# Routing of two top-2 expert layers moved into the loops that make their inputs, with pair lists in DRAM and weights loaded per expert

## What is computed

```python
x = x + gnn0(norm(x))      # node softmax * row softmax of (h @ h.T masked by adj), times x @ weight, + bias
x = x + ffn0(norm(x))      # 8 experts, top 2 of x @ Wg + bg; silu(x @ w1) * (x @ w3) @ w2, hidden 512
x = x + gnn1(norm(x))      # relu((adj @ x) @ W.T + b)
x = x + ffn1(norm(x))      # 8 experts, top 2 of x @ gate_w.T; gelu(x @ w1.T + b1) @ w2.T + b2, hidden 1024
# routing of both expert layers:
top_vals, top_idx = top_k(logits, 2);  gates = softmax(top_vals)
y = sum over the two chosen experts of gate * expert(x)
```

## Time and profile before

| | us |
|---|---|
| median of 3 runs | 1865.2 (1862.47 to 1866.99) |
| the profiled execution, own time | 1865.87 |
| its span, first to last instruction | 1864.2 |
| TensorE's mean granted clock, of full speed | 0.927 |
| PE, DVE, ACT, POOL busy in the span | 1550.2, 1156.6, 639.2, 651.3 |
| PE instructions, DVE instructions | 9584, 3520 |

### The profile page before, as it was taken

The page is one execution under the profiler, slowest core; times in us unless marked ns, Lnnn a source line. Parts: engine busy times, 40 slices in busy tenths (PEclk is TensorE's granted clock), DMA queues, the critical chain, the costliest instruction groups (busy, mean ns, idle before and its releaser), DMA issues. The chain is left out here.

```text
span 1864.2 us, 35268 instructions
## 1 busy us (share of the span) xinstructions
PE 1550.2 (83%) x9584; PEld 1295.2 (69%) x9584; DVE 1156.6 (62%) x3520; ACT 639.2 (34%) x1367; POOL 651.3 (35%) x1336
## 2 busy tenths in 40 slices
PE   5899999999999718999996079999259999999990
PEld 4788888888888607888785045555138888888880
DVE  5466677776677685555653837666765655566543
ACT  2333333333333302333332523222014454454544
POOL 0123233222332105555553014333224444445530
PEclk9899999999999958999999579999669999999995
DMA  7224433344333171111112744655501111111119
GB/s 116 87 109 149 156 134 127 131 147 158 134 127 126 60 271 43 51 52 49 52 51 78 250 146 160 212 190 179 214 24 34 37 37 34 37 34 37 39 30 296
DMA packets 91017, 204.73 MB, mean 110 GB/s; under 512 B 13792, under 2 KB 64481, under 8 KB 87009
## 3 DMA queue, kind: packets, MB, share of 16 engines
q1 hardware_dynamic: 74368, 148.15, 23.8%
q0 software_dynamic: 11328, 30.95, 5.3%
q10 hardware_dynamic: 5280, 25.17, 3.4%
HBM read 146.17 MB, written 58.08 MB: 110 GB/s over the span
## 5 line engine op out<-in xcount | busy, mean ns | idle before, releaser
L1128 PE MATMUL bank<-ffn_w_in_parts,ffn_x_t 128*128 128x512 f32 x1416 | 359.7, 402 | 1.4 <-DVE ffn_w_in_parts L1254 1.4
L1152 PE MATMUL bank<-ffn_w_out_parts,ffn_hidden_t 128*128 128x256 f32 x2124 | 285.5, 289 | 26.2 <-DVE ffn_hidden_t L1244 26.2
L1128 PEld LDWEIGHTS bank<-ffn_w_in_parts,ffn_x_t 128*128 128x128 f32 x1416 | 259.2, 190 | 54.7 <-DVE ffn_w_in_parts L1254 4.4
L1152 PEld LDWEIGHTS bank<-ffn_w_out_parts,ffn_hidden_t 128*128 128x128 f32 x2124 | 264.2, 193 | 30.5 <-DVE ffn_w_out_parts L1254 19.2
L623 PE MATMUL bank<-h_t,attn_h_tile 128*128 128x512 f32 (+1 forms) x1092 | 248.9, 383 | 3.9 <-POOL attn_h_tile L492 3.9
L658 PE MATMUL bank<-support,attn_probs_t 128*128 128x512 f32 x650 | 246.6, 412 | 2.8 <-DVE attn_probs_t L532 2.6
L623 PEld LDWEIGHTS bank<-h_t,attn_h_tile 128*128 128x128 f32 x1092 | 196.9, 189 | 46.2 <-issue 4.1
L520 ACT CAST attn_probs_t<-bank 128x512 fp32r<-128x512 f32 (+1 forms) x182 | 98.7, 557 | 351.9 <-PE bank L632 351.9
L1194 ACT ACTIVATE ffn_silu_or_gelu<-bank,w_b_in 128x128 f32<-128x128 f32 x472 | 134.7, 368 | 202.4 <-PE bank L1139 202.4
L660 PE MATMUL bank<-support,attn_probs_t 128*128 128x256 f32 x676 | 184.9, 280 | 0.0
L1244 DVE TENSOR_TENSOR ffn_hidden_t<-ffn_silu_or_gelu,ffn_hidden_t 128x512 fp32r<-128x512 f32 x118 | 81.1, 692 | 138.3 <-ACT ffn_hidden_t L1200 123.0
(11 more groups left out here) (245 smaller groups left out, 2414.5 us busy)
## 6 DMA issues: line engine op xcount, KB each, us to landing
adj_tile<-in_adj SPq DMA_DIRECT2D x25, 1663.5 KB, 21.6
mask<-attn_mask ACTq DMA_DIRECT2D x26, 832.0 KB, 3.4
nbr_mask<-mask SPq DMA_DIRECT2D x26, 832.0 KB, 5.2
comb_y<-y SPq DMA_DIRECT2D x12, 768.0 KB, 10.3
w_w_in<-in_w SPq DMA_DIRECT2D x16, 512.0 KB, 10.3
w_w_in<-in_w_t SPq DMA_DIRECT2D x16, 512.0 KB, 4.3
comb_x<-x SPq DMA_DIRECT2D x6, 768.0 KB, 10.5
w_w_out<-in_w SPq DMA_DIRECT2D x1, 4096.0 KB, 20.0
```

The costliest lines, as they stand in the source:

```text
L1128: ins = pe.matmul(bank[2 + 2 * slot + b][:, :], XT[:, slot, xp, k, :], WIP[:, wp, k, b * CH:(b + 1) * CH], start=n == 0 and k == 0, stop=n ...
L1152: ins = pe.matmul(bank[7][:, 0:D], HTT[:, hp, k, :], WOP[:, wp, k, :], start=n == 0 and k == 0, stop=n == 2 and k == KH - 1)
```

## The change

Both `route` stages are removed. Their work is done per row tile by new methods of `Gate` inside `attend` and `neighbours`:

- `pick` (DVE): the top two of the 8 logits of a row by the 8-wide maximum and index instructions, and which experts the row uses.
- `count` (PE): two matmuls with 8 columns, the rank of each pair within its tile and the tile's totals; the result lies in a corner of bank 2 (attend) or 5 (neighbours).
- `rank` (DVE): adds the running base of each expert and takes out the two places of each row. An expert's list has room for all rows (`CAP`), so a place is known at once.
- `scatter` (POOL): two indirect DMAs of 128 pairs of integers, 8 bytes each, to the list `pairs` in DRAM.
- `plan` (DVE, once at the end): for each of the 59 tiles its expert and the row of `pairs` where it begins.

In `attend` PE's scores of chunk 2 wait for `ranks_read` and `count` stands at group 3 of a step. In `neighbours` `count` stands first in a step, ACT converts all four groups (`odd` moves from DVE), one bank less is used for the transposed sum, and the last step does `add` and `finish` ahead of the last logits. `experts` reads each tile's list with a small DMA by SP (a register load and a DMA per tile), and the weights are loaded there, expert by expert, by ACT, ahead of `copy_x(0)`; DVE waits for one expert's weights at a time (8 tiles are written out ahead of its loop). In ffn1 the first matrix is still loaded in `neighbours`. The empty lists are filled in `project`.

```diff
 class Gate:
+    def pick(self, dve, t, slot):
+        dve.wait_ge(self.logits_ready, t + 1)
+        dve.memset(self.TAKER[:, E + 1:E + 2], 0.0)
+        link(dve.max(self.M8[:, slot, :], self.L[:, slot, :]))
+        dve.tensor_tensor(self.r["gates"][:, 1, bass.ds(t, 1)], self.M8[:, slot, 1:2], self.M8[:, slot, 0:1],
+                          ALU.subtract).then_inc(self.diff_ready, 1)
+        link(dve.max_index(self.I8[:, slot, :], self.M8[:, slot, :], self.L[:, slot, :]))
+        link(dve.tensor_copy(self.EF[:, slot, :], self.I8[:, slot, 0:2]))
+        link(dve.tensor_scalar(self.OH[:, slot, :], self.k["IE"][:], self.EF[:, slot, 1:2], None, ALU.is_equal))
+        dve.scalar_tensor_tensor(self.USED[:, slot, :], ...).then_inc(self.used_ready, 1)
+    def count(self, pe, t, slot, rows=P):
+        pe.wait_ge(self.used_ready, t + 1)
+        pe.wait_ge(self.ranks_read, t)
+        pe.matmul(self.PS[:, 0:E], self.k["BEFORE"][0:rows, :], self.USED[0:rows, slot, :], start=True, stop=True)
+        pe.matmul(self.PS[:, E:2 * E], self.k["ONES"][0:rows, :], self.USED[0:rows, slot, :], ...).then_inc(self.ranked, 1)
+    def rank(self, dve, t, uses, slot):
+        dve.wait_ge(self.ranked, t + 1)
+        link(dve.tensor_tensor(self.A[:], self.PS[:, 0:E], base, ALU.add))
+        dve.tensor_tensor(self.BASE[:, 1 - slot, :], self.PS[:, E:2 * E], base, ALU.add).then_inc(self.ranks_read, 1)
+        for k in range(2):
+            link(dve.scalar_tensor_tensor(self.JUNK[:, k, :], ..., accum_out=self.SLF[:, slot, k:k + 1]))
+        dve.tensor_copy(self.SLI[:, slot, :], self.SLF[:, slot, :]).then_inc(self.slots_ready, 1)
+    def scatter(self, pool, t, uses, slot, rows=P):
...
+        for k in range(2):
+            pool.indirect_dma_start(out=self.pairs, out_offset=..., in_=self.VALS[0:rows, slot, k, :], ...)
+    def plan(self, dve):
...
@@ attend, DVE, step
                         rest(t, slot, [g])
                         ...
+                    gate.rank(dve, t - 2, uses - 1, slot)
                     if not (first and slot == 0):
                         gate.logits(dve, t - 1, 1 - slot)
+                        gate.pick(dve, t - 1, 1 - slot)
@@ attend, PE
+                        if c == 2 and (not known(t) or t >= 4):
+                            pe.wait_ge(gate.ranks_read, t - 3)
...
+                        if g == 3 and (not known(t) or t >= 2):
+                            pe.wait_ge(masked, T * NC if last else (t + 2) * NC)
+                            gate.count(pe, t - 2, slot)
-def route(nc, bank, name, LG, r, w, load):
...
@@ class Weights
+    def load(self, act):
         if self.b_in is not None:
+            act.dma_start(self.BI[:], self.b_in).then_inc(self.b_loaded, 16)
+            act.dma_start(self.BO[:], self.b_out.partition_broadcast(P)).then_inc(self.b_loaded, 16)
+        m = self.w_in.shape[2] // E
+        for e in range(E):
+            if not self.early:
+                act.dma_start(self.WI[:, :, e * m:(e + 1) * m], self.w_in[:, :, e * m:(e + 1) * m]).then_inc(self.in_loaded[e], 16)
+            act.dma_start(self.WO[:, :, e * D:(e + 1) * D], self.w_out[:, :, e * D:(e + 1) * D]).then_inc(self.out_loaded[e], 16)
@@ experts, SP
+                    row = sp.value_load(r["row"][0:1, bass.ds(t, 1)], min_val=0, max_val=LIST_TILES - 1)
+                    sp.dma_start(PAIRS[:, bass.ds(t * 2, 2)], pairs[bass.ds(row * P, P), :]).then_inc(pairs_in[slot], 16)
@@ experts, ACT
+                w.load(act)
                 copy_x(0, 0, 0)
@@ neighbours, POOL, step
+                        gate.scatter(pool, t - 3, uses - 2 + slot, 1 - slot)
                     gate.norm(pool, t, uses, slot)
```

More of the change, by code:

```diff
@@ L39 @@
 PAIR_ROWS = 2 * NP
+CAP = T * P
+LIST_TILES = 240
+assert LIST_TILES >= S + (E - 1) * (T - 1)
 def tiles(eng, count, step, head=2):
@@ L604, in _ @@
                 link(dve.tensor_scalar(NATT[:], NATT[:], NSM[:, 3:4], None, ALU.mult))
-                tiles(dve, T, step)
+                tiles(dve, T, step, head=4)
+                gate.rank(dve, T - 2, (T - 2) // 2, T % 2)
                 gate.sums(dve, T - 1, (T - 1) % 2, range(E))
                 gate.logits(dve, T - 1, (T - 1) % 2)
+                gate.pick(dve, T - 1, (T - 1) % 2)
+                gate.rank(dve, T - 1, (T - 1) // 2, (T - 1) % 2)
+                gate.plan(dve)
             @block.tensor
@@ L667, in _ @@
                 scores(0, 0, True)
-                tiles(pe, T, step)
+                tiles(pe, T, step, head=4)
+                gate.count(pe, T - 2, T % 2)
+                gate.count(pe, T - 1, (T - 1) % 2, TAIL)
 def combine(nc, a, bank, x_in, gates, x_out, parts):
@@ L1324, in _, with neighbours @@
                     split_w_in(1, 2, b)
-                tiles(dve, S, step)
-def neighbours(nc, a, bank, XH, gate_w, LG, w):
+                tiles(dve, S, step, head=E)
+def neighbours(nc, a, bank, XH, gate_w, r, w):
     sizes = (7, 7, 6, 6)
@@ L1392, in _, with step @@
                 gate.constants(pool)
-                tiles(pool, T, lambda t, uses, slot, first, last: gate.norm(pool, t, uses, slot))
+                def step(t, uses, slot, first, last):
+                    if not known(t) or t >= 3:
+                        gate.scatter(pool, t - 3, uses - 2 + slot, 1 - slot)
+                    gate.norm(pool, t, uses, slot)
+                tiles(pool, T, step, head=6)
+                gate.scatter(pool, T - 3, (T - 3) // 2, (T - 3) % 2)
+                gate.scatter(pool, T - 2, (T - 2) // 2, (T - 2) % 2)
+                gate.scatter(pool, T - 1, (T - 1) // 2, (T - 1) % 2, TAIL)
+                gate.scattered_all(pool)
             @block.tensor
@@ L1449, in _ @@
                 pe.wait_ge(w_loaded, 32)
-                tiles(pe, T, step)
+                tiles(pe, T, step, head=6)
             @block.scalar
@@ L1464, in even, with odd @@
                     act.activation(AT[:, 0, 0:w], bf[0][:, 0:w], ACT.Copy, bias=1.0, scale=1.0 / BIG).then_inc(at_ready, 1)
+                def odd(t, slot, g, first):
+                    act.wait_ge(flipped, t * G + g + 1)
+                    if not (first and slot == 0 and g < 2):
+                        act.wait_ge(used, t * G + g - 1)
+                    w = GS[g][1] * P
+                    act.activation(AT[:, 1, 0:w], bf[1][:, 0:w], ACT.Copy, bias=1.0, scale=1.0 / BIG).then_inc(at_odd, 1)
                 def tail(t, slot, first):
@@ L1475, in flip_out @@
                         act.wait_ge(out_done, t - 1)
[L1476 removed]
+                    act.copy(AGT[:, slot, :, :], bank[4][:, 0:D].rearrange("p (k n) -> p k n", k=KD)).then_inc(agt_ready, 1)
                 def step(t, uses, slot, first, last):
[L1479 to L1483 removed]
+                    very_first = first and slot == 0
+                    even(t, slot, 0, first)
+                    if not very_first:
+                        tail(t - 1, 1 - slot, first)
+                    odd(t, slot, 1, first)
+                    even(t, slot, 2, first)
+                    if not very_first:
                         flip_out(t - 1, 1 - slot, first)
+                    odd(t, slot, 3, first)
                     if last:
@@ L1574, in build @@
             w.place_out(while_used)
-            route(nc, bank, "gate0", LG, r, w, w.load)
-            experts(nc, a, bank, "ffn0", w, H0, r)
+            experts(nc, a, bank, "ffn0", w, H0, r, a["pairs"][0])
         with ExitStack() as while_used:
```

436 lines of the change are left out of this document (203 added, 233 removed).

## The result

The changed kernel took **1919.6 us** (median of 4 runs, 1917.9 to 1927.7), the kernel before 1863.8 beside it: ratio 1.031, 95% interval 1.0289 to 1.033 (the two medians by themselves give 1.030). It is 3.1% slower; 1856.5 was forecast, 1827 to 1880. The profiled execution has a span of 1916.2 us against 1864.2, so 52.0 us are to be found.

The account below looks back on a forecast made before the run. PE was taken to bound the attention loop and mostly the neighbour loop, DVE the route stages. Terms -13.3 - 11.4 + 7 + 9 = -8.7 us took 1865.9 to 1857.2, and the median 0.7 under it to 1856.5; range 1827 to 1880.

Parts of the forecast that it names:

- What throttles the issuer: Expert stages: a queue holds about 1690 rows, so ACT's weight issues take 26.2 us; first product at 27.4, in ffn1 25.4.
- Rival (a): Expert stages: ACT isn't held by its queue, first products come 15.3 and 13.6 us earlier than forecast; 1827.6 us, chance 0.13.
- The tail of attend: Last attention logits to first expert product: 10.4 us of work, a 0.96 barrier, then 27.4; product 13.3 us earlier than before.
- scatter lies beside plan: End of attend: POOL's last scatters, 2 x 1.03 us and a landing, about 4.5 us, run beside DVE's 5.2 us plan.
- The tail of neighbours: End of neighbours to ffn1's first product: rows end 2.8 us sooner, three tiles 18.4, plan 5.2; product 11.4 us earlier.
- What the attention loop pays: Attention loop: added PE work and waits 0.17 us, DVE stalls 0.1 us a tile, over 26 tiles +7 us.
- rival (b): Both routed loops pay next to nothing: count fits between transposes, DVE stays in its room; 1840.5 us, chance 0.12.
- PE's waits for the masked sum under 5 us: Attention loop, sign in the profile after: PE's waits for DVE's masked sum stay under 5 us in total.
- 2.25 us of room, and 0.54 of idle time before the result: Attention loop: DVE's slack, by which an odd step takes 2.8 us of added work for nothing, an even one 3.2.
- Rival (c): Both routed loops: DVE becomes the bound, its twelve added instructions cost 3.6 us a tile, 24 us in all; 1880, chance 0.25.
- the port, for POOL's scatters in neighbours: Neighbours loop: POOL's scatters exclude DVE instructions with two SBUF inputs and lengthen DVE's sums, one way to the 1880 us case.
- Expert loops, "nothing": Expert loops, combine and project: no added cost, as SP's list read runs ahead of the 5.4 us of a tile.

Follow-up runs that it names:

- e4_loads_spread: Changed kernel, with ACT's weight loads spread over its first steps (three experts ahead of the first copy) instead of all eight first: 1900.9 us, ratio 1.0209.
- e8_plan_late: Changed kernel, with DVE starting plan at the end of both routed loops only when POOL has issued the last two scatters: 1918.8 us, a single run.
- f3_full_rows: Changed kernel, with the last tile's scatters given 128 rows instead of 127, the 128th sent to two unread places: 1913.4 us, ratio 1.0261.
- e1_adj_ahead: Changed kernel, with the adjacency load issued one tile earlier in SP's order in the attention loop: 1877.3 us, ratio 1.0089.

## Why the prediction was wrong

Two steps failed: that a later result in attention costs nothing (39.7 us of the miss), and that the scatters at the end of both routed loops lie beside plan (7.2 and 8 us). By its own steps, in its order:

- **What throttles the issuer: right.** The queue of ACT, which no row had shown full, behaved like SP's. 26.0 us of issues against 26.2, product at 27.4 against 27.4; in the second stage 24.9 from ACT's first issue against 25.4. Rival (a) is out, and e4_loads_spread shows that the wait was ACT's and could be avoided.
- **The tail of attend: short by 7.2 us.** From the last logits to the plan 2.7 us (3.1 forecast), but plan took 7.7 for 5.2, and behind it 8.0 us passed to the next stage where I had put a barrier of 0.96. These terms alone are 9.1 us over; 2.1 of the forecast's 10.4, the later last result, are counted in the loop here. The step that failed is "scatter lies beside plan", with 2 x 1.03 us and a landing, about 4.5: plan and barrier were put on the path, and the scatters are what the stage waits for, as e8_plan_late shows. Two of its terms were too small. The issues take 3.04 + 2.72 us for 2 x 1.03, a duration from scatters of 128 rows where the last tile has 127; f3_full_rows gives that back, 3.7 us. And from the end of the issues to the next stage 8.5 to 8.9 us pass in the three runs, where the forecast has 2.4 for the landing and 0.96 for the barrier. The kernel before has 3.6 us there behind its last scatter of result rows (1818.27 to 1821.85). Why the small pairs take 5 us longer no run shows.
- **The tail of neighbours: short by 8 us for the same reasons**, 32.6 us from the last rows (1368.35) to the next stage instead of 24.6: the three tiles of logits 17.0 for 18.4 (by its own terms the forecast's sum is 3 x 6.2 = 18.6), plan 7.7 for 5.2, and 8 for a barrier of 1. The loop gave 3 of it back: from the first to the last of DVE's sums with the bias (L1507, now L1527) it is 4.2 us longer (220.9 for 216.7), with the start 1.4 shorter, against +9 less 2.8. Rank and pick cost 2.2 us, not 3.0.
- **What the attention loop pays: wrong, +46.7 for +7** (rival (b), that the loops pay next to nothing, is out with it), from the first result to the last (572.1 for 525.4). The terms themselves held: DVE's added work was smaller than said, and with the collision away (e1_adj_ahead) the loop is 4.7 us longer, near the 7. The sign that the prediction named, PE's waits for the masked sum under 5 us, came true as well; it looked at the wrong wait. The step that failed is the one that gave DVE "2.25 us of room, and 0.54 of idle time before the result" and let the result move inside it for nothing. Two things hang on the result that were not asked: SP's store, the adjacency load behind it and POOL's conversion behind that. The prediction followed the instructions that were added, and not what a later result moves. What the runs showed in its place: 36.0 us of waits for the splits, about 6 us of lower clock, and the 4.7.
- **Rival (c)** had the side, but half the size of attention's loss (24 us over both loops), and another mechanism: its condition, twelve instructions of 3.6 us, was not met (2.2). Beside it stood the port, for POOL's scatters in neighbours, without the condition that the Trainium skill (SBUF — State Buffer, section SBUF: two separate sides) puts on a product with two SBUF inputs, that the GpSimd instruction reads SBUF. There it did next to nothing (gate products 435 ns for 428; one at 1375.23 took its 0.42 us inside a scatter's issue, 1375.10 to 1376.29). It was visible in attention, in the kernel before, as a mean that two equal instructions don't share:

```profile
L223 DVE CUSTOM_DVE_ANT_0 attn_gate_products<-attn_x_normed,attn_gate_w 128x256 f32<-128x256 f32 x208 | 96.1, 500 | 3.4 <-issue 3.4
```

```profile
L223 DVE CUSTOM_DVE_ANT_0 nbr_gate_products<-nbr_x_normed,nbr_gate_w 128x256 f32<-128x256 f32 x208 | 75.6, 428 | 1.0 <-issue 1.0
```

  72 ns over 8 products are 0.6 us a tile, all of it in one product, 0.3 us short of where PE begins to wait.
- **Expert loops, "nothing": 3.8 and 5.0 us.** The diff showed a wait for every expert's weights ahead of each half; 24 a change were priced at zero, and are 3.0 us of the first loop.

## What to carry over

Before a delay is called free because its engine has room, follow everything that is released by the late instruction, through the queues that stand behind it, and ask what it will meet where it arrives. A mean that differs between two instructions of the same shape (500 and 428 ns) is a collision already under way; look up what runs beside its longest one, and how far it is from the point where somebody waits. Let an engine that others wait for issue only as many loads as its queue takes at once, and load a streamed input one tile further ahead than seems needed: it cost nothing before, and was worth 42 us after. When two things end a stage side by side, ask which one lands last, and take its landing from a transfer of the same kind.

## What the runs showed of the hardware

- One product with two SBUF inputs waited out a whole POOL instruction (3.17 us beside 3.21), and beside four shorter ones two products waited for one each (1.09 us).
- An indirect DMA of 127 rows took POOL 2.55 to 3.04 us to issue, one of 128 rows at the same place in the program 0.96 and 1.06 (0.95 to 1.32 over the 104 of f3_full_rows). Other numbers of rows weren't tried.
- The next stage began 7.4 to 8.9 us behind the end of POOL's last scatter of 8-byte pairs (both seams of the changed kernel, e8_plan_late and f3_full_rows), and 3.6 us behind the last scatter of 1 KB rows in the kernel before.
- While POOL issued such a one of 127 rows, two of DVE's float32 `tensor_scalar` instructions on SBUF, of 59 and 26 columns, stood still until its end (1.74 and 1.52 us; 0.18 each when it was absent). One of 8 columns at 704.30 did not (0.16 us).
- ACT's queue held its issuer as SP's does: 26.0 us for 16 transfers of 6144 rows in all, the first four issues of which took 0.63 to 0.79 us each.
- Four times, shortly after a wait of 1.7 to 1.9 us, PE's matmuls slowed for about 3 us (0.63 for 0.39 us each; granted clock 0.97 over 210 us).
- A wait on a satisfied semaphore cost DVE 21 to 26 ns, here 24 of them at each change of expert.
